# A selective scan beside two feed-forward blocks: odd decays in SBUF instead of PSUM, wide products, later attention steps

## Chip, cores, metric

The kernel runs on one core of a Trainium2 chip. The metric is the device time of one launch in microseconds, the median of several runs. TensorE is called PE here, VectorE DVE, ScalarE ACT, GpSimd POOL, SyncE SP.

## What is computed

Four samples of 512 tokens by 512 channels go through four residual steps. Cut to what matters:

```python
# 1: selective scan over the context (ctx: 4 x 512 x 256), 512 channels, 16 states
u  = silu(causal_conv4(ctx @ in_proj.T) + conv_b)            # channels x time
dt = softplus(dt_proj @ (x_proj[:16] @ u) + dt_b)
B, C = x_proj[16:32] @ u, x_proj[32:48] @ u                  # 16 x time each
state[n] = exp(-exp(A_log[:, n]) * dt) * state[n] + dt * u * B[n]      # over time
y  = (sum_n state[n] * C[n] + D * u) * silu(layernorm(x))
x += tanh(g_xattn[0]) * y.T
# 2: feed-forward 512 -> 2048 -> 512 with ternary weights and 8-bit tokens, exact gelu
x += tanh(g_ffn[0]) * bitlinear(gelu(bitlinear(layernorm(x), w1)), w2)
# 3: channel attention: q, k from ctx; A = softmax(q k^T) (512 x 512)
x += tanh(g_xattn[1]) * (layernorm(x) @ A.T)
# 4: fp32 feed-forward 512 -> 2048 -> 512 with biases, exact gelu
x += tanh(g_ffn[1]) * (gelu(layernorm(x) @ proj1.T + b1) @ proj2.T + b2)
```

## The kernel before

**Passes.** Five passes over a hand-written order of 15 slots. Pass 0 does the scan and attention matrix of sample 0, beside the quantisation of the weights. Three looped passes do steps 2 to 4 (called `rest`, sample b) beside the scan (called `scans`, sample b + 1). The last one does steps 2 to 4 of the last sample with three-product fp32. Every engine runs through the same slots; semaphores tie them.

**The scan.** Channels lie on partitions: four tiles of 128, so a state n is two half states, s = 2n + p, of two rows (q = 0, 1) of 128 x 512. `SCAN_SLOTS` puts state 0 into slot 4, two states into each of slots 5 to 11, and state 15 into slot 12. For a half state:

- POOL forms the state input `work[s % 6] = du * bcast` (L1541), four half states ahead, after it has issued the accumulation of an earlier half (`u += work`, a DMA that adds, L1552). Two accumulations into the same half of `u` follow one another, each waiting for the landing of the one before.
- ACT forms the decays, `exp(a_neg * dt)`, one instruction a row, in PSUM tile `pairs[s % 2]` (L811), once `s_hc` says that the half state two before has been multiplied. It also copies the rows of B and C, which PE has broadcast into a PSUM bank with a one-column matmul (L424), to `bcast` and `ccast` (L796).
- DVE scans each row in place in the PSUM pair, with `work` as addend (L1168, L1181), and multiplies by `ccast` back into `work`. In pass 0 and outside slots 5 to 8 the product is wide: both rows at once, 1024 elements (L1173). In slots 5 to 8 of the looped passes each row's product follows its scan (L1185), so that ACT is released row by row.

**Beside it in slots 5 to 8** of a looped pass: four up-products a slot of step 4 (`f_up`, L603, eight matmul instructions each, banks 2 and 3 in turn) and their gelus on ACT (L1026) in pairs. Gelu and exponential need different tables, so ACT loads a table four times a slot. Slots 9 to 14 have the down-products (L616).

**The attention matrix** of the next sample: in slots 6 to 9 PE forms the energies of a quarter (L481), DVE takes the maximum (L1288) after the slot's second half state, ACT the exponential with its sum (L944), DVE the reciprocal (L1348) after the third, ACT the probabilities (L949); PE transposes (L436) and ACT copies (L933) one slot later.

**Other users.** `xn` (two rows of 512, fp32) holds normalised tokens of step 4 (`norm_apply`, L1364), transposed by PE until slot 4; in slots 9 and 10 it takes the unneeded output of the statistics of `x` (L954, L958), and in slot 12 silu(layernorm(x)) (`gates_silu`, L973), with which DVE multiplies y (L1305) after `last_sum` (L1295) has waited for the last accumulations. POOL adds the second bias to the residual in slots 4 and 5 (L1609).

Of the kernel before, what the change touches and what calls it, by code (L numbers as in the profile page):

```python
# [10 lines left out]
ALU = mybir.AluOpType  # L11
# [36 lines left out]
GELU_SLOTS = (5, 6, 7, 8)  # L48
# [3 lines left out]
ATT_LAST_SLOT = 10  # L52
ZSTAT_SLOT = 10
ZS_SLOT = 12
GATE_SLOT = 13
QUANT_SLOT = 14
# [24 lines left out]
def state_at(slot, which):  # L81

    return SCAN_SLOTS[slot][which] if slot in SCAN_SLOTS else None

# [26 lines left out]
def program(nc, x_d, ctxT_d, ipw_d, xpw_d, dtw_d, pch_d, w1_d, w2_d, wqk_d, bqk_d, ffn_d, b1_d, b2_d, gate_d,  # L111
            ident_d, identb_d, pick_d, out_d):
    with ExitStack() as ctx:
# [301 lines left out]
        def _(pe):  # L415
# [249 lines left out]
            def middle(b, m, prev, scans, rest):  # L665

                if not rest:
                    pe.wait_ge(s_const, const_wait)
                    pe.wait_ge(s_ones, 2)
                if rest:  # L670
                    up1(b, 3, range(FC - 1))
                    down1(b, 1)
                    up1(b, 3, (FC - 1,))
                    norm_transpose(b, 0)
                    transpose_h(b, 2)
                if scans:
                    low_rank(m)
                if rest:
                    down1(b, 2)
                    norm_transpose(b, 1)  # L680
                    transpose_h(b, 3)
                if scans:
                    step_sizes(m, prev)
                if rest:
                    down1(b, 3)
                    attend(b, 0)
                if scans:
                    scan_bcast(m, 0, 0)
                if rest:
                    norm_transpose(b, 2)  # L690
                    attend(b, 1)
                if scans:
                    scan_bcast(m, 1, 0)
                if rest:
                    norm_transpose(b, 3)
                    attend(b, 2)
                if scans:
                    scan_bcast(m, 0, 1)

            def pass_(b, scans, rest=True):  # L700

                m, prev = (b + 1, b) if rest else (0, None)
                for slot in range(SLOTS if scans else 5):
                    if slot == 3:
                        middle(b, m, prev, scans, rest)
                    if scans and slot == QUANT_SLOT:
                        turn(m, prev)
                        continue
                    if scans and slot == 0:
                        project(m, prev, 0)  # L710
                        project(m, prev, 1)
                    if rest:
                        if slot == 0:
                            up1(b, 2)
                        if slot == 4:
                            norm_transpose(b, 4)
                            attend(b, 3)
                            norm_transpose(b, 5)
                    if scans:
                        if slot == 0:  # L720
                            project(m, prev, 2)
                        if slot == 1:
                            project(m, prev, 3)
                        bcast_next(m, slot, 0, 0)
                        if slot in ATT_SLOTS and ATT_SLOTS[slot]:
                            att_transpose(m, ATT_SLOTS[slot] - 1)
                        if slot == ATT_LAST_SLOT:
                            att_transpose(m, J - 1)
                        if slot == QK_SLOT:
                            qk_products(m, prev, 0)  # L730
                    if rest and slot == GATE_SLOT:
                        f_unit(b, slot, 0)
                    if scans and slot == GATE_SLOT:
                        gate_transposes(m, range(T))
                    if rest:
                        if slot == 1:
                            down1(b, 0)
                        if slot < 2:
                            transpose_h(b, slot)
                        if slot != GATE_SLOT:  # L740
                            f_unit(b, slot, 0)
                    else:
                        weights(slot)
                    if scans:
                        bcast_next(m, slot, 0, 1)
                        if slot in ATT_SLOTS:
                            energies(m, ATT_SLOTS[slot])
                        if slot == QK_SLOT:
                            qk_products(m, prev, 1)
                    if rest:  # L750
                        if slot == 4:
                            norm_transpose(b, 6)
                            norm_transpose(b, 7)
                        f_unit(b, slot, 1)
                    if scans:
                        bcast_next(m, slot, 1, 0)
                    if rest:
                        f_unit(b, slot, 2)
                    if scans:
                        bcast_next(m, slot, 1, 1)  # L760
                    if rest:
                        f_unit(b, slot, 3)
                if not scans:
                    tail(b)
# [13 lines left out]
            pass_(None, True, rest=False)  # L778
            with pe.Fori(0, B - 1) as i:
                pass_(i, True)  # L780
            pass_(B - 1, False)


        @block.scalar
        def _(act):
# [17 lines left out]
            def decay_half(b, s):  # L803

                n, p = divmod(s, 2)
                if n == 0:
                    act.wait_ge(s_dt, b * 2 + p + 1)
                for q in range(HALF):
                    if n:
                        act.wait_ge(s_hc, (b * HN + s - DECAYBUFS) * HALF + q + 1)  # L810
                    act.activation(pairs[s % DECAYBUFS][:, q, :], dt[:, p * HALF + q, :], ACT.Exp,  # L811
                                   scale=a_neg[:, p * HALF + q, n:n + 1]).then_inc(s_decay, 1)

            def decays(b, prev, slot, which, part):

                n = state_at(slot, which)
                if n is not None:
                    if n == 0 and part == 0:
# [3 lines left out]
                        decay_half(b, 0)  # L822
                    if n == 0 and part == 0 and prev is not None:
                        act.wait_ge(s_x3, prev * T + T)
                    if 2 * n + 1 + part < HN:
                        decay_half(b, 2 * n + 1 + part)
# [76 lines left out]
            def middle(b, m, prev, scans, rest):  # L903
                if not rest:
                    set_up()
                    for _, i, c in W_EARLY:
                        square(i, c)
                if rest:
                    gelu1(b, 3)
                    norm_copy(b, 0)  # L910
                    h_copy(b, 2)
                if scans:
                    low_rank_copy(m, prev)
                if rest:
                    norm_copy(b, 1)
                    h_copy(b, 3)
                if scans:
                    softplus(m, prev)
                    first_copy(m, prev, 0, 0)
                if rest:  # L920
                    norm_copy(b, 2)
                if scans:
                    first_copy(m, prev, 1, 0)
                if rest:
                    norm_copy(b, 3)
                if scans:
                    first_copy(m, prev, 0, 1)
# [806 lines left out]
```

## Time and profile before

| what | us |
|---|---|
| median of 3 runs (1079.14 to 1080.04) | 1079.6 |
| profiled execution, its own time | 1083.82 |
| its span | 1082.0 |
| busy: PE, DVE, ACT, POOL | 819.5, 838.0, 666.3, 574.1 |
| mean granted PE clock, of full speed | 0.882 |
| state inputs, POOL L1541, 128 | 350.6, 2.773 each |
| scans, DVE L1168 and L1181, 256 | 186.9 and 117.5 |
| products, DVE L1173 wide, 80, and L1185 narrow, 96 | 98.0 and 66.4 |
| decays, ACT L811, 256 | 166.0 |

Busy shares are means over stages that are limited in different ways, so the table names the candidates only. A mean for a POOL instruction contains the time in which it overlaps the issue of a DMA.

### The profile page before, as it was taken

To read this page: it belongs to the slowest core of one execution; us is meant where nothing else is said; L and a number is where in the kernel's file an instruction comes from. 1 tells how busy PE (TensorE), PEld (TensorE's weight loads), DVE (VectorE), ACT (ScalarE), POOL (GpSimd) and SP (SyncE) were. 2 spreads that over 40 slices of the span, in tenths; PEclk is the share of its full clock that TensorE was granted. 3 is DMA by queue.
4 is the path that set the end of the run, shared out by engine and by line. 5 is a ranking of instruction groups with operands and counts; after the bars stand their busy time and mean duration, and the time that the engine had idled before them with its cause. 6 is when DMAs were issued, how large, how long until landed. Compare 5 with 4: busy or idle time off the path is not lost.

```text
span 1082.0 us, 10856 instructions
## 1 busy us (share of the span) xinstructions
PE 819.5 (76%) x2664; PEld 403.2 (37%) x2704; DVE 838.0 (77%) x999; ACT 666.3 (62%) x969; POOL 574.1 (53%) x495
## 2 busy tenths in 40 slices
PE   4432310689699987989699988879799987887997
PEld 1110010344334334444333434443333333445886
DVE  3889868887988897787988898777888997655332
ACT  4678869375489952565589852555599851523442
POOL 0497786124797783134997781125996871232000
PEclk8655555798899998998899999998899998998999
DMA  7059985001189996201299994201398993200221
GB/s 269 0 98 206 250 170 111 0 1 40 19 187 204 199 230 172 91 8 39 45 197 203 205 235 124 98 1 39 70 207 179 220 229 86 98 0 20 98 98 59
DMA packets 51429, 129.99 MB, mean 120 GB/s; under 512 B 6304, under 2 KB 7456, under 8 KB 50864
## 3 DMA queue, kind: packets, MB, share of 16 engines
q0 software_dynamic: 17280, 62.92, 31.6%
q1 hardware_dynamic: 34096, 66.53, 17.9%
q14 instruction: 41, 0.34, 0.1%
q8 instruction: 12, 0.20, 0.1%
HBM read 62.33 MB, written 4.19 MB: 61 GB/s over the span
## 4 chain that ended last, share of the span: by engine, by line
PE 27%; DVE 22%; issue 14%; ACT 12%; DMA 11%; POOL 7%; DVEq 1%; ACTq 0%; POOLq 0%
DMA u<-work 11%; DVE pair L1168 6%; PE bank L631 4%; PE pair L631 4%; POOL work L1541 4%; PE pair L515 3%; PE bank L616 3%; DVE pair L1181 3%; PE pair L543 2%; ACT pair L811 2%; ACT L811 2%; PE pair L592 2%; PE bank L603 2%; ACT L1026 1%; PE bank L450 1%
## 5 line engine op out<-in xcount | busy, mean ns | idle before, releaser
L1541 POOL TENSOR_TENSOR work<-du,bcast 128x1024 f32<-128x1024 f32 x128 | 350.6, 2773 | 12.8 <-ACT bcast L796 7.7
L811 ACT ACTIVATE pair<-dt,a_neg 128x512 f32<-128x512 f32 x256 | 166.0, 683 | 69.7 <-DVE work L1173 53.5
L1168 DVE TENSOR_TENSOR_SCAN pair<-pair,work 128x512 f32<-128x512 f32 x160 | 186.9, 1214 | 15.4 <-ACT pair L811 11.7
L603 PE MATMUL bank<-stage,ring 128*128 128x512 f32 x384 | 174.8, 598 | 11.5 <-ACT stage L1026 3.7
L1552 POOL DMA_DIRECT2D u<-work x120 | 129.7, 1081 | 66.3 <-DMA u<-work 25.1
L1181 DVE TENSOR_TENSOR_SCAN pair<-pair,work 128x512 f32<-128x512 f32 x96 | 117.5, 1224 | 25.2 <-ACT pair L811 24.8
L424 PE MATMUL bank<-xd,pick 128*128 128x512 bf16 x108 | 48.6, 450 | 114.3 <-ACT bcast L796 74.1
L603 PEld LDWEIGHTS bank<-stage,ring 128*128 128x128 f32 x384 | 70.4, 189 | 96.0 <-issue 78.2
L1173 DVE TENSOR_TENSOR work<-pair,ccast 128x1024 f32<-128x1024 f32 x80 | 98.0, 1225 | 10.4 <-DVE pair L1168 4.7
L616 PE MATMUL bank<-ring,stage 128*128 128x512 f32 x192 | 85.4, 595 | 9.0 <-DVE stage L1406 7.7
L424 PEld LDWEIGHTS bank<-xd,pick 128*128 128x128 bf16 x128 | 12.9, 100 | 171.5 <-ACT bcast L796 110.0
L1185 DVE TENSOR_TENSOR work<-pair,ccast 128x512 f32<-128x512 f32 x96 | 66.4, 691 | 5.4
L543 PE MATMUL pair<-w2q,hx 128*128 128x512 bf16 x242 | 63.9, 416 | 7.7 <-issue 4.1
L515 PE MATMUL pair<-w1q,qT 128*128 128x512 bf16 x250 | 60.4, 387 | 12.2 <-ACT qT L979 7.1
L1192 DVE SCALAR_TENSOR_TENSOR u<-xpad,pch,u 128x512 f32<-128x512 f32 x48 | 40.6, 850 | 25.1 <-ACT u L837 23.9
L1527 POOL TENSOR_SCALAR fst<-fst 128x1 f32<-128x1 f32 x32 | 12.9, 404 | 87.5 <-DVE fst L1356 86.9
L592 PE MATMUL pair<-attT,stage 128*128 128x512 f32 x128 | 57.6, 592 | 0.0
L979 ACT ACTIVATE qT<-bank 128x512 bf16<-128x512 bf16 x16 | 9.5, 593 | 77.3 <-PE bank L502 77.3
L616 PEld LDWEIGHTS bank<-ring,stage 128*128 128x128 f32 x192 | 35.8, 190 | 51.4 <-issue 51.3
L796 ACT ACTIVATE bcast<-bank 128x512 f32<-128x512 f32 x64 | 37.2, 582 | 22.3 <-PE bank L424 17.7
L796 ACT ACTIVATE ccast<-bank 128x512 f32<-128x512 f32 x64 | 37.3, 584 | 13.7 <-PE bank L424 13.3
L616 PE MATMUL bank<-ring,hT 128*128 128x512 f32 x96 | 45.7, 621 | 0.0
(177 smaller groups left out, 1635.3 us busy)
## 6 DMA issues: line engine op xcount, KB each, us to landing
u<-work POOLq DMA_DIRECT2D x120, 512.0 KB, 5.8
ring<-ffn_dram SPq DMA_DIRECT2D x144, 256.0 KB, 4.9
ring<-ffn_dram SPq DMA_DIRECT2D x16, 512.0 KB, 3.3
xres<-x_dram SPq DMA_DIRECT2D x4, 1024.0 KB, 5.4
stage<-w_dram SPq DMA_DIRECT2D x1, 4096.0 KB, 16.5
stage<-w_dram SPq DMA_DIRECT2D x4, 1024.0 KB, 7.0
out_dram<-stage SPq DMA_DIRECT2D x16, 256.0 KB, 2.3
ctxT<-ctxT_dram SPq DMA_DIRECT2D x4, 512.0 KB, 6.5
```

The source lines that it names most:

```text
L515: last = pe.matmul(banks[4 + g % 3][:], qT[:, k, t * P:(t + 1) * P], w1q[:, k, c * 512:(c + 1) * 512], start=k == 0, stop=k == J - 1)
L543: last = pe.matmul(banks[7][:], hqT[:, f, :], w2q[:, f, :], start=f == 0, stop=f == FT - 1)
L592: last = pe.matmul(banks[ATT_BANKS[t]][:], xnT[:, k, t * P:(t + 1) * P], attT[:, k, :], start=k == 0, stop=k == J - 1)
L603: last = pe.matmul(banks[2 + f % 2][:], piece(f)[:, k * P:(k + 1) * P], xnT[:, k, :], start=k == 0, stop=k == J - 1)
L616: last = pe.matmul(banks[2 + t % 2][:], h_tile(f)[:, t * P:(t + 1) * P], piece(k), start=f == 0, stop=f == FT - 1)
L631: out = pe.matmul(bank[:], in_parts(weights), in_parts(moving), start=first and i == 0, stop=last and i == len(parts) - 1)
L811: act.activation(pairs[s % DECAYBUFS][:, q, :], dt[:, p * HALF + q, :], ACT.Exp, scale=a_neg[:, p * HALF + q, n:n + 1]).then_inc(s_decay, 1)
L1168: dve.tensor_tensor_scan(pair[:, q, :], pair[:, q, :], rows[:, q, :], 0.0, ALU.mult, ALU.add).then_inc(s_scan, 1)
L1173: dve.tensor_tensor(rows, pair[:], ccast[:, n % 2, :].unsqueeze(1).broadcast_to([P, HALF, L]), ALU.mult).then_inc(s_hc, HALF)
L1181: dve.tensor_tensor_scan(state, state, row, 0.0, ALU.mult, ALU.add).then_inc(s_scan, 1)
L1541: pool.tensor_tensor(work[:, s % SCANBUFS, :, :], du[:, p * HALF:(p + 1) * HALF, :], bcast[:, n % 2, :].unsqueeze(1).broadcast_to([P, HALF ...
L1552: pool.dma_start(u[:, p * HALF:(p + 1) * HALF, :], work[:, s % SCANBUFS, :, :], accum_op=ALU.add).then_inc(s_acc[p], 16)
```

## The change

The order of the slots before slot 4 is written out as three functions on each engine (`opening`, `between`, `closing`), in the order that the slots gave before. What differs otherwise:

- The decays of the odd half states of states 1 to 15 go to `xn` in SBUF. DVE scans from `xn` into the PSUM pair. ACT forms them at the end of the half slot before, ahead of the gelus, once `s_scan` says that the odd half before has been scanned row by row.
- All products are wide.
- The attention steps move: energies after the slot's second up-product, the maximum after the third half state, the exponential at the end of the slot and the reciprocal after the fourth half; probabilities, transposes and copy in the next slot.
- The statistics' unneeded output goes to `q1`; `gates_silu` also waits for the last scan.

```diff
+SPARE_STATES = range(1, 16)
+def spare(n, p):
+    return p == 1 and n in SPARE_STATES
...
             def decay_half(b, prev, s):
                 n, p = divmod(s, 2)
                 if n == 0:
                     act.wait_ge(s_dt, b * 2 + p + 1)
+                dst = xn if spare(n, p) else pairs[s % DECAYBUFS]
+                if spare(n, p) and n == SPARE_STATES[0] and prev is not None:
+                    act.wait_ge(s_xnT, prev * 2 * T + 2 * T)
                 for q in range(HALF):
-                    if n:
+                    if spare(n, p):
+                        if n > SPARE_STATES[0]:
+                            act.wait_ge(s_scan, (b * HN + s - 2) * HALF + q + 1)
+                    elif n:
                         act.wait_ge(s_hc, (b * HN + s - DECAYBUFS) * HALF + q + 1)
-                    act.activation(pairs[s % DECAYBUFS][:, q, :], dt[:, p * HALF + q, :], ACT.Exp,
+                    act.activation(dst[:, q, :], dt[:, p * HALF + q, :], ACT.Exp,
                                    scale=a_neg[:, p * HALF + q, n:n + 1]).then_inc(s_decay, 1)
...
+            def decays_ahead(b, prev, slot, which):
+                n = state_at(slot, which)
+                if n is not None and spare(n + 1, 1):
+                    decay_half(b, prev, 2 * (n + 1) + 1)
...
             def gates_silu(b):
                 act.wait_ge(s_emm, b * J + J)
+                act.wait_ge(s_scan, (b * HN + 2 * SPARE_STATES[-1] + 2) * HALF)
```

ACT's slot afterwards (from slot 4 on; `m` is the scan's sample):

```python
decays(m, prev, slot, 0, 0)               # nothing where the odd half is a spare one
if slot == 4: decays(m, prev, slot, 0, 1); norm_copy(b, 5)
copy_next(m, slot, 0, 0); quarter(m, slot, 0, rest)
if slot - 1 in ATT_SLOTS: energy_probs(m, ATT_SLOTS[slot - 1])
if slot == QK_SLOT: qk_copy(m, prev, 0)
if slot != 4: decays(m, prev, slot, 0, 1)
copy_next(m, slot, 0, 1); quarter(m, slot, 1, rest)
if slot - 1 in ATT_SLOTS: att_copy(m, prev, ATT_SLOTS[slot - 1])
if slot == QK_SLOT: qk_copy(m, prev, 1); norm_copy(b, 6); norm_copy(b, 7)
decays_ahead(m, prev, slot, 0)
f_gelus(b, slot, 0)
copy_next(m, slot, 1, 0); quarter(m, slot, 2, rest)
decays(m, prev, slot, 1, 1); copy_next(m, slot, 1, 1)
if slot in ATT_SLOTS: energy_exp(m, ATT_SLOTS[slot])
quarter(m, slot, 3, rest)
decays_ahead(m, prev, slot, 1)
f_gelus(b, slot, 2)
if slot == ZS_SLOT: gates_silu(m)
```

PE's: `bcast_next(0, 0)`, `f_unit 0`, `att_transpose(slot - 1)`, `bcast_next(0, 1)`, `f_unit 1`, `energies(slot)`, `bcast_next(1, 0)`, `f_unit 2`, `bcast_next(1, 1)`, `f_unit 3`. DVE's half state and slot:

```diff
-            def half_step(b, prev, n, p, wide):
+            def half_step(b, n, p):
...
+                source = xn if spare(n, p) else pairs[s % DECAYBUFS]
+                rows = work[:, s % SCANBUFS, :, :]
+                pair = pairs[s % DECAYBUFS]
                 for q in range(HALF):
                     done = (b * HN + s) * HALF + q + 1
                     dve.wait_ge(s_decay, done)
-                    dve.tensor_tensor_scan(state, state, row, 0.0, ALU.mult, ALU.add).then_inc(s_scan, 1)
...
+                    dve.tensor_tensor_scan(pair[:, q, :], source[:, q, :], rows[:, q, :], 0.0,
+                                           ALU.mult, ALU.add).then_inc(s_scan, 1)
...
-                        energy_max(m, slot)
...
+                    half(m, prev, slot, 1, 0)
+                    energy_max(m, slot)
+                    half(m, prev, slot, 1, 1)
+                    if slot in ATT_SLOTS:
+                        energy_sum(m, slot)
```

## Rows read from the trace of the kernel before

**Rows 1.** Windows: length, busy PE, PEld, DVE, ACT, POOL, clock, DMA share, GB/s.

```profile
530.20:566.00 35.80, 33.42 (x82) 14.79 (x82) 30.25 (x35) 29.32 (x43) 35.37 (x23) 0.95 0.80 170
583.90:601.80 17.90, 16.70 (x42) 7.04 (x43) 15.52 (x20) 16.61 (x25) 13.05 (x8) 1.00 0.84 173
617.60:632.10 14.50, 12.88 (x36) 5.91 (x36) 13.90 (x14) 10.46 (x21) 13.06 (x13) 1.00 1.06 256
```

**Rows 2.** Timeline of ACT in a gelu slot: start, us, instruction, [idle before].

```profile
345.12 1.28 ACT L1026 ACT_TABLE_LOAD   x1
346.42 1.27 ACT L1026 ACTIVATE hT<-bank,b 128x512 f32<-128x512 f32 x2
...
349.00 1.30 ACT L811 ACTIVATE pair<-dt,a_neg 128x512 f32<-128x512 f32 x2
350.24 0.57 ACT L796 ACTIVATE bcast<-bank 128x512 f32<-128x512 f32 x1
...
354.17 0.69 ACT L944 ACTIVATE xd<-bank,ast 128x512 f32<-128x512 f32 x1 [1.17 <-DVE ast L1288]
```

**Rows 3.** Timeline of DVE in gelu slots.

```profile
353.46 0.68 DVE L1288 TENSOR_REDUCE ast<-bank 128x1 f32<-128x512 f32 x1
...
359.56 1.23 DVE L1181 TENSOR_TENSOR_SCAN pair<-pair,work 128x512 f32<-128x512 f32 x1 [1.54 <-ACT pair L811]
360.83 0.69 DVE L1185 TENSOR_TENSOR work<-pair,ccast 128x512 f32<-128x512 f32 x1
```

**Rows 4.** Timeline of PE in a gelu slot.

```profile
339.13 3.70 PE L603 MATMUL bank<-stage,ring 128*128 128x512 f32 x8 [0.88 <-ACT hT L1026]
342.84 0.39 PE L424 MATMUL bank<-xd,pick 128*128 128x512 bf16 x1
...
351.35 1.13 PE L481 MATMUL bank<-xpad 128*128 128x512 f32 x2
```

**Rows 5.** Single lines of DVE: duration in ns, least, median, most.

```profile
L1168 DVE TENSOR_TENSOR_SCAN pair<-pair,work x160: 1199/1208/1232, 51.5 to 891.7; 128x512 f32<-128x512 f32 x160
...
L1173 DVE TENSOR_TENSOR work<-pair,ccast x80: 1223/1225/1226, 53.9 to 893.0; 128x1024 f32<-128x1024 f32 x80
...
L1225 DVE TENSOR_TENSOR dt<-dt,hT x4: 1224/1224/3247, 47.1 to 752.2; 128x1024 f32<-128x1024 f32 x4
...
L1192 DVE SCALAR_TENSOR_TENSOR u<-xpad,pch,u x48: 744/751/2344, 12.9 to 709.4; 128x512 f32<-128x512 f32 x48
```

**Rows 6.** Timelines of POOL and DVE where both work in SBUF.

```profile
45.97 3.25 POOL L1541 TENSOR_TENSOR work<-du,bcast 128x1024 f32<-128x1024 f32 x1 [2.42 <-DVE du L1227]
47.07 3.25 DVE L1225 TENSOR_TENSOR dt<-dt,hT 128x1024 f32<-128x1024 f32 x1
...
225.59 2.32 POOL L1602 TENSOR_SCALAR du<-du,fst 128x2048 f32<-128x2048 f32 x1 [9.45 <-DVE fst L1373]
...
287.15 0.54 DVE L1364 TENSOR_SCALAR xn<-stage,fst 128x512 f32<-128x512 f32 x1
287.37 0.87 POOL L1504 TENSOR_SCALAR u<-u,pch 128x512 f32<-128x512 f32 x1
287.60 0.92 DVE L1364 TENSOR_SCALAR xn<-stage,fst 128x512 f32<-128x512 f32 x1
```

**Rows 7.** Timelines of POOL and DVE, gelu slot and slot 9.

```profile
360.75 2.35 POOL L1541 TENSOR_TENSOR work<-du,bcast 128x1024 f32<-128x1024 f32 x1 [1.24 <-ACT bcast L796]
...
375.52 1.21 DVE L1168 TENSOR_TENSOR_SCAN pair<-pair,work 128x512 f32<-128x512 f32 x1
376.64 1.20 DVE L1168 TENSOR_TENSOR_SCAN pair<-pair,work 128x512 f32<-128x512 f32 x1
376.82 2.67 POOL L1541 TENSOR_TENSOR work<-du,bcast 128x1024 f32<-128x1024 f32 x1
```

**Rows 8.** Waits of DVE: total us, times, longest.

```profile
DVE u L1295 <- DMA u<-work: 10.9, 6, 2.8
```

**Rows 9.** Timeline of POOL in pass 0.

```profile
92.71 0.88 POOL L1552 DMA_DIRECT2D u<-work  x1 [3.00 <-DMA u<-work]
```

More of the change, by code:

```diff
@@ L51 @@
 ATT_SLOTS = {6: 0, 7: 1, 8: 2, 9: 3}
-ATT_LAST_SLOT = 10
 ZSTAT_SLOT = 10
@@ L700, in pass_, with opening @@
[L700 to L706, printed above, removed]
+            def opening(m):
+                for j in range(J):
+                    project(m, None, j)
+                pe.wait_ge(s_const, const_wait)
+                pe.wait_ge(s_ones, 2)
+                low_rank(m)
+                step_sizes(m, None)
+                scan_bcast(m, 0, 0)
+                scan_bcast(m, 1, 0)
+                scan_bcast(m, 0, 1)
@@ L707, in pass_ @@
+            def pass_(b, rest=True):
+                m, prev = (b + 1, b) if rest else (0, None)
+                if rest:
+                    between(b, m)
+                else:
+                    opening(m)
+                for slot in range(4, SLOTS):
+                    if slot == QUANT_SLOT:
                         turn(m, prev)
                         continue
-                    if scans and slot == 0:
-                        project(m, prev, 0)
-                        project(m, prev, 1)
+                    bcast_next(m, slot, 0, 0)
+                    if slot == QK_SLOT:
+                        qk_products(m, prev, 0)
@@ L712, in pass_ @@
                     if rest:
[L713 to L730, printed above, removed]
@@ L742, in pass_ @@
                     else:
                         weights(slot)
[L744 to L751, printed above, removed]
+                    if slot - 1 in ATT_SLOTS:
+                        att_transpose(m, ATT_SLOTS[slot - 1])
@@ L901, in tail, with opening @@
                         weight_high(b, f + 2)
[L903 to L927, printed above, removed]
+            def opening(m):
+                for j in range(J):
+                    project_copy(m, None, j)
+                silu_u(m)
+                set_up()
+                for _, i, c in W_EARLY:
+                    square(i, c)
+                low_rank_copy(m, None)
+                softplus(m, None)
+                first_copy(m, None, 0, 0)
+                first_copy(m, None, 1, 0)
+                first_copy(m, None, 0, 1)
@@ L1467, in pass_ @@
+                dve_m.start()
+                if rest:
+                    between(b, m)
+                else:
+                    opening(m)
+                for slot in range(4, SLOTS):
+                    half(m, prev, slot, 0, 0)
+                    if rest and slot == 4:
+                        norm_apply(b, 6)
+                        norm_apply(b, 7)
+                    half(m, prev, slot, 0, 1)
                     if rest and (slot, 0) in FOURTH_SLOTS:
                         fourth(b, FOURTH_SLOTS[slot, 0])
[L1469 to L1474 removed]
+                    half(m, prev, slot, 1, 0)
+                    energy_max(m, slot)
+                    half(m, prev, slot, 1, 1)
+                    if slot in ATT_SLOTS:
+                        energy_sum(m, slot)
+                    mixer_last(m, prev, slot)
@@ L1679, in _ @@
-            pass_(None, True, rest=False)
+                pool_m.start()
+                if rest:
+                    between(b, m)
+                else:
+                    softplus_log(m)
+                    start_sum(m, None)
+                for slot in range(4, SLOTS):
+                    if rest and slot == 5:
+                        bias(b, 2)
+                    half(m, prev, slot, 0, 0)
+                    if rest and slot == 4:
+                        bias(b, 0)
+                    if rest and slot == 5:
+                        bias(b, 3)
+                    half(m, prev, slot, 0, 1)
+                    if rest and slot == 4:
+                        bias(b, 1)
+                    if not rest:
+                        weights(slot)
+                    half(m, prev, slot, 1, 0)
+                    half(m, prev, slot, 1, 1)
+                    mixer_last(m, slot)
```

536 lines of the change are left out of this document (261 added, 275 removed).

## Prediction

> **What bounds the kernel now.** I read the windows by stage first. In one of the three looped passes, slots 5 to 8, each with two states (four half states) beside four up-products and their gelus, take 17.9 us in slot 8 (slots 5 and 6 together 35.8), and no engine is idle for much of that: PE 16.7, ACT 16.6, DVE 15.5. Slot 10 takes 14.5 us, 3.62 per half state, with DVE at 13.9 [rows 1]. So DVE sets slots 9 to 12; what sets a gelu slot has to be found in the queues.
>
> ACT's timeline of a gelu slot gives steps from start to start: table load 1.29, two gelus 1.28, a half state's two exponentials 1.24, a copy 0.48, the energies' exponential 0.80 [rows 2]; the probabilities take about as long as that, 0.73. Four loads, two gelu pairs, four half states, four copies, an attention copy, probabilities and exponential make 16.6 us. The missing 1.2 is the wait for DVE's maximum [rows 2]. DVE itself waits 1.54 for decays [rows 3]. ACT and DVE thus feed each other through the two PSUM pairs: this is the wait the change is aimed at. PE waits 0.88 for a gelu [rows 4].
>
> **The change, part by part, if nothing new collides.** *Wide products:* two narrow ones of 0.69 [rows 3] become one of 1.225 [rows 5], so the 96 narrow ones of the three passes, as 48 wide, save 7.5 us of DVE time, but only where DVE sets the pace. *Decays ahead:* instruction count and table loads stay the same (exponentials, gelus, exponentials, gelus in a slot), so ACT's 16.6 us stays the floor. *Attention:* the same instructions in other places, nothing added. *Moved statistics output* to q1: free, q1 is idle then.
>
> The new order closes another ring. From the first gelu at a slot's end it is 0.74 until PE starts, f_up 3.71, transposes 0.43, broadcast 0.24, f_up 3.47, energies 0.96, broadcast 0.24, f_up 3.47, last broadcast 0.49 to its landing [rows 4] (an f_up right behind a broadcast is 3.47 from start to start); then on ACT the copy 0.48, energies' exponential 0.80, decays ahead 1.24, table load 1.29 [rows 2]. Sum 17.6 us against 17.9. Laid out from slot 4 (the table loads and decays of the first slot included), slot 9 starts 2.4 us earlier than before. After it DVE's 3.62 per half state is unchanged. Three passes: 7 us.
>
> Queues behind new waits: on ACT the odd decays now wait for the previous odd half's scans (s_scan), and the gelus, and behind them PE's next up-products, are queued behind that. gates_silu now waits for the last scan; then a table load and two silus (1.3 + 1.4) against DVE's product and sum (2.3): 0.5 us per pass at most. POOL's instructions and DMAs (30 accumulations a pass) keep their order.
>
> **The collision.** The scan of an odd half today reads a PSUM pair and work. Afterwards it reads xn and work, both in SBUF, while POOL's state input reads du and bcast. What such a pair does is in the trace. A DVE tensor_tensor with both inputs in SBUF, 1.224 us at its shortest and in the middle, took 3.25 us when POOL's state input had been issued before it [rows 5, 6]; and that state input, else 2.35 [rows 7], took 3.25, held up by the DVE instruction before. In the convolution, all operands in SBUF, one step of 0.75 took 2.34 beside POOL's rounding [rows 5, 6]. Against that, 160 scans and 80 wide products with one input in PSUM lie within 1.199 to 1.232 and 1.223 to 1.226 us, with POOL at work beside most of them [rows 5]. So the two exclude each other for whole instructions when DVE has two inputs in SBUF. The Trainium skill says the same (SBUF — State Buffer, "Who interferes with whom": a DVE instruction with two SBUF inputs contends with a GpSimd instruction that reads SBUF); the trace agrees, 3.25 against 1.224. Without rule and rows alike the sum would be the 1072 of the first rival. No scan of that kind is in the trace: its price lies between 0 and a whole state input, 2.34, for each scan; I take the lock, since the nearest rows are two-input instructions too.
>
> Who goes first? Two DVE instructions in a row do not keep POOL out: between norm_apply's two, POOL's waiting multiply of 0.87 came through, and the second took 0.92 where the first took 0.54 [rows 6]. So first come, first served. A product's end releases both the next scan and POOL's accumulation with the state input behind it: scans at 375.52 and 376.64, the input at 376.82 [rows 7]. On time, the input thus comes 0.18 us after the second scan and merely waits ("a near miss", some 0.5 us per state); if the first scan starts 0.2 us late, or energy_max (0.68 [rows 3]) sits before it, the input slips between the scans and the second waits 2.34 ("a hit"). A near miss leaves POOL late by half a microsecond, which makes the next one a hit: they alternate.
>
> *Slots 5 and 6.* POOL is behind after the bias adds (35.4 of 35.8 us busy [rows 1]) and always has something waiting. Odd halves 3, 5, 7, 9 then pay 1.3 + 2.35, 1.25 + 1.55, 0.5 + 2.35 and 2.35: 11.6 us. Eight half states of 3.6, a wait of 1.3 for the first decays, a maximum of 0.6 and these give 42.3 us against 35.8. ACT's gelus wait with it, as their decays stand before them: slot 7 starts 6.4 later.
>
> *Slots 7 and 8.* State inputs of even halves wait for ACT's broadcast copy (today 1.24 us [rows 7]) and so come after both odd scans: no hits. DVE needs 15.0 us, catches up in slot 7 (16.3), and slot 8 takes the ring's 17.6. 33.9 against 35.8: slot 9 starts 4.5 later.
>
> *Slots 9 to 12.* I get hits at halves 21, 25 and 29 (the first through energy_max, the others by alternation): 7.0, with near misses 0.5. POOL's last inputs, for halves 30 and 31, come late behind its gate statistics, so that one of them still meets half 29; after that it has none left. Today DVE waits at the end for the accumulations, 10.9 us in six waits, two in each of the three passes [rows 8]; 3.6 a pass; later half states give the accumulations that time, 3.1 with the silus' 0.5 taken off. Net 4.4.
>
> *Pass 0.* Thirteen odd halves collide too, but POOL itself waits there for accumulations (3.00 us and more [rows 9]), and runs 6 to 12 us behind DVE; most is swallowed. I count 4 us (0 to 15).
>
> Sum: 3 × (4.5 + 4.4) + 4 = 30.7 us, 31 in whole microseconds. The profiled execution took 1083.8 us (span 1082.0, 1.8 around it), 4.2 above the median of 1079.6; the same 31 on the median gives **1110 us**.
>
> **Rivals.** *No collision for scans* (faster side): then the ring gain alone stands: 7 us, 1072. For it: no scan with two SBUF inputs was seen. Against: three kinds of two-input or fast DVE instruction collide. It decides if odd scans stay at 1.21 us. *The pair of scans stays together*: no hits, only waits of up to 1.2 for a running input; slots 5 and 6 lose about 3, later slots 0.5 per state, the end gives 3 back: 1080 to 1086. The deciding point is whether POOL comes between two queued scans. *Every odd half is hit* up to half 27: three more hits in slots 9 to 11 (7.0), 4 in slots 7 and 8 beyond their slack of 2.6, and 5 in pass 0: 38 more, 1148. *The changed order alone costs*: PE's last broadcast of a slot stands behind energies and an up-product; if ACT and PE drift, the 17.6 becomes 18.5, 10 us over the passes; it would show without any long scan.
>
> **Chances and range.** Collision with alternation 0.60 (1095 to 1128 of its own); every half hit 0.10; scans together 0.13, half of it within what I call the same; no collision 0.14; order alone 0.03. A difference below 0.2% (2 us) cannot be told from none here: faster 0.14, same 0.06, slower 0.80. The range, 1076 to 1138, leaves out most of the no-collision case and the upper half of the worst one.
>
> **What would show it.** By form, the scans with xn as input: maximum near 3.5 us, mean above 1.8, scans with pair inputs still 1.21. State inputs up to 2.34 + 1.2. Half states of slots 9 to 11 in pairs of 7.7 and 9.5 us instead of 7.2. Slot 5 plus 6 at 42 us, slot 7 at 16. Narrow products gone; ACT waiting on s_scan before its odd decays in slots 5 and 6. I would be wrong if odd scans lie at 1.21 us, or if pass 0 grew by more than 15 us.

## The result, and the profile after

The changed kernel takes 1203.5 us (four runs, 1201.7 to 1204.9) against 1079.8: a ratio of 1.1125, 95% interval 1.1067 to 1.1182. It is 11% slower, 124 us where 31 were forecast, and above the range's 1138. The profiled execution took 1201.7 us, with a span of 1199.9.

The page of the changed kernel: busy time and share by engine, then the costliest groups.

```profile
PE 850.7 (71%) x2704; PEld 416.6 (35%) x2704; DVE 1000.3 (83%) x951; ACT 672.1 (56%) x969; POOL 589.1 (49%) x495
...
L1589 POOL TENSOR_TENSOR work<-du,bcast 128x1024 f32<-128x1024 f32 x128 | 345.1, 2698 | 4.8 <-DVE du L1248 4.8
L1200 DVE TENSOR_TENSOR_SCAN pair<-xn,work 128x512 f32<-128x512 f32 x120 | 318.5, 2698 | 5.6 <-ACT xn L831 5.6
...
L1205 DVE TENSOR_TENSOR work<-pair,ccast 128x1024 f32<-128x1024 f32 x128 | 156.8, 1225 | 18.6 <-DVE pair L1200 9.1
L1200 DVE TENSOR_TENSOR_SCAN pair<-pair,work 128x512 f32<-128x512 f32 x136 | 158.7, 1213 | 3.5 <-ACT pair L831 3.0
L831 ACT ACTIVATE xn<-dt,a_neg 128x512 f32<-128x512 f32 x120 | 84.4, 718 | 90.5 <-DVE pair L1200 90.3
```

The single line of the scans: duration in ns, least, median, most.

```profile
L1200 DVE TENSOR_TENSOR_SCAN pair<-pair,work x136: 1199/1210/1232, 51.7 to 1016.3; 128x512 f32<-128x512 f32 x136
L1200 DVE TENSOR_TENSOR_SCAN pair<-xn,work x120: 1199/1390/12783, 64.9 to 1019.9; 128x512 f32<-128x512 f32 x120
```

The 136 scans from PSUM kept their time; the 120 from `xn` went from 1.21 us [rows 5] to a mean of 2.70, with one of 12.8. That is 120 × (2.698 - 1.21) = 179 us more in the scans. DVE's busy time grew by 162: busy time counts once where two rows overlap, and two narrow products had cost more than a wide one. POOL's state inputs have not grown: 2.70 after, 2.77 before. One side pays all. ACT's decays waited 90 us for those scans, and the gelus and PE's up-products with them. PE's granted clock fell to 0.85 (0.88 before) and its busy time rose by 31 us; in the first kernel below, where only the scans' source differs, the clock is 0.877 and the loss is gone.

Windows of pass 2, cut at the starts of half states 2, 10, 18 and 31 (columns as in [rows 1]):

```profile
587.13:637.41 50.28, 37.65 (x86) 16.19 (x84) 47.73 (x27) 30.57 (x44) 35.91 (x23) 0.87 0.64 131
637.41:677.72 40.31, 32.85 (x84) 14.31 (x84) 39.11 (x31) 33.74 (x49) 26.23 (x16) 1.00 0.78 170
677.72:744.10 66.38, 54.22 (x115) 23.51 (x116) 64.38 (x45) 34.05 (x62) 44.88 (x40) 0.85 0.80 183
```

The same stretches of the kernel before are 35.86, 35.75 and 49.79 us long. DVE is now busy for 95 to 97% of all three. From start to start of half state 0, pass 0 grew by 25.6 us (232.0 to 257.6), the first two looped passes by 31.1 and 33.7, and the third with all behind it by 27.2. No stretch was spared.

Half state 3, where the largest loss sits. Single rows of DVE, POOL and ACT's timelines; an x1 row is one instruction:

```profile
591.88 12.62 DVE L1200 TENSOR_TENSOR_SCAN pair<-xn,work 128x512 f32<-128x512 f32 x1 [0.99 <-ACT xn L831]
604.42 1.20 DVE L1200 TENSOR_TENSOR_SCAN pair<-xn,work 128x512 f32<-128x512 f32 x1
...
591.75 1.54 POOL L1657 TENSOR_TENSOR stage<-stage,b 128x512 f32<-128x512 f32 x1
592.97 1.19 POOL L1600 DMA_DIRECT2D u<-work  x1
593.59 2.94 POOL L1589 TENSOR_TENSOR work<-du,bcast 128x1024 f32<-128x1024 f32 x1
...
598.95 3.24 POOL L1589 TENSOR_TENSOR work<-du,bcast 128x1024 f32<-128x1024 f32 x1
601.25 2.15 POOL L1657 TENSOR_TENSOR stage<-stage,b 128x512 f32<-128x512 f32 x1
...
604.54 0.72 ACT L831 ACTIVATE xn<-dt,a_neg 128x512 f32<-128x512 f32 x1 [8.61 <-DVE pair L1200]
```

A scan of 1.21 us waited until POOL had worked off all that was ready in its queue: two state inputs and four bias additions, the last of which ended at 603.40, 1.10 us before the scan did. They stand back to back but for 0.30 us (593.29 to 593.59), in which only an accumulation was being issued; the scan did not get its turn there either.

The steady state, slot 6, single rows of DVE and POOL:

```profile
609.75 1.23 DVE L1205 TENSOR_TENSOR work<-pair,ccast 128x1024 f32<-128x1024 f32 x1 [0.20 <-DVE pair L1200]
610.89 1.39 DVE L1200 TENSOR_TENSOR_SCAN pair<-xn,work 128x512 f32<-128x512 f32 x1
612.19 3.82 DVE L1200 TENSOR_TENSOR_SCAN pair<-xn,work 128x512 f32<-128x512 f32 x1
...
608.53 2.65 POOL L1589 TENSOR_TENSOR work<-du,bcast 128x1024 f32<-128x1024 f32 x1
611.64 0.89 POOL L1600 DMA_DIRECT2D u<-work  x1 [0.46 <-issue]
612.26 2.65 POOL L1589 TENSOR_TENSOR work<-du,bcast 128x1024 f32<-128x1024 f32 x1
```

The product's end at 610.98 releases both sides. The first scan meets the tail of the input before (608.53 + 2.65 = 611.18) and takes 1.39 instead of 1.21. The second is thereby issued 0.07 us ahead of the next input, not 0.18 as forecast, and ends when that input has ended: 3.82 us. In this way every odd half of slots 5 to 8 behind half 3 is hit, 1.39 + 3.82 or, behind a maximum, about 4.6 in all, against 2.42 without a hit. Slot 8 takes 20.2 us and slot 10 21.0 (657.56 to 677.72 and 697.88 to 718.89, from scan to scan), against 17.90 and 14.50 [rows 1].

### The profile page after: what moved, and what is told of

It reads as the page before. It is cut to its first block, busy times and chain, and to the rows that moved or that the text cites. A ratio compares the mean times of both kernels' runs of the same rounds, so it can differ in the third digit from the quotient of the medians.

```text
span 1199.9 us, 10941 instructions
## 1 busy us (share of the span) xinstructions
PE 850.7 (71%) x2704; PEld 416.6 (35%) x2704; DVE 1000.3 (83%) x951; ACT 672.1 (56%) x969; POOL 589.1 (49%) x495
## 4 chain that ended last, share of the span: by engine, by line
PE 31%; DVE 29%; issue 13%; ACT 6%; POOL 2%; DVEq 1%; ACTq 0%; POOLq 0%
DVE pair L1200 18%; PE bank L607 7%; PE bank L635 4%; PE pair L635 4%; PE pair L519 3%; PE bank L620 3%; PE pair L547 2%; PE pair L596 2%; ACT L1082 2%; PE bank L454 1%; DVE hx L1438 1%; DVE fst L1430 1%; DVE fst L1413 1%; PE bank L477 1%; DVE u L1213 1%
## 5 line engine op out<-in xcount | busy, mean ns | idle before, releaser
L1200 DVE TENSOR_TENSOR_SCAN pair<-xn,work 128x512 f32<-128x512 f32 x120 | 318.5, 2698 | 5.6 <-ACT xn L831 5.6
L607 PE MATMUL bank<-stage,ring 128*128 128x512 f32 x384 | 185.2, 627 | 56.0 <-ACT stage L1082 41.0
L1600 POOL DMA_DIRECT2D u<-work x120 | 116.4, 970 | 177.9 <-DVE work L1205 148.9
L1205 DVE TENSOR_TENSOR work<-pair,ccast 128x1024 f32<-128x1024 f32 x128 | 156.8, 1225 | 18.6 <-DVE pair L1200 9.1
L1200 DVE TENSOR_TENSOR_SCAN pair<-pair,work 128x512 f32<-128x512 f32 x136 | 158.7, 1213 | 3.5 <-ACT pair L831 3.0
L831 ACT ACTIVATE xn<-dt,a_neg 128x512 f32<-128x512 f32 x120 | 84.4, 718 | 90.5 <-DVE pair L1200 90.3
L428 PE MATMUL bank<-xd,pick 128*128 128x512 bf16 x128 | 57.2, 447 | 109.4 <-ACT bcast L810 66.1
L831 ACT ACTIVATE pair<-dt,a_neg 128x512 f32<-128x512 f32 x136 | 88.3, 682 | 76.9 <-DVE work L1205 60.8
L620 PE MATMUL bank<-ring,stage 128*128 128x512 f32 x192 | 97.4, 663 | 17.9 <-ACT hx L1082 9.2
L440 PE MATMUL bank<-ident,xd 128*128 128x128 f32 x64 | 13.2, 343 | 42.3 <-ACT xd L1004 42.3
```

Source lines behind the costliest of these rows:

```text
L607: last = pe.matmul(banks[2 + f % 2][:], piece(f)[:, k * P:(k + 1) * P], xnT[:, k, :], start=k == 0, stop=k == J - 1)
L620: last = pe.matmul(banks[2 + t % 2][:], h_tile(f)[:, t * P:(t + 1) * P], piece(k), start=f == 0, stop=f == FT - 1)
L831: act.activation(dst[:, q, :], dt[:, p * HALF + q, :], ACT.Exp, scale=a_neg[:, p * HALF + q, n:n + 1]).then_inc(s_decay, 1)
L1200: dve.tensor_tensor_scan(pair[:, q, :], source[:, q, :], rows[:, q, :], 0.0, ALU.mult, ALU.add).then_inc(s_scan, 1)
L1205: dve.tensor_tensor(rows, pair[:], ccast[:, n % 2, :].unsqueeze(1).broadcast_to([P, HALF, L]), ALU.mult).then_inc(s_hc, HALF)
L1600: pool.dma_start(u[:, p * HALF:(p + 1) * HALF, :], work[:, s % SCANBUFS, :, :], accum_op=ALU.add).then_inc(s_acc[p], 16)
```

## The experiments

Theory 1 is the collision: the whole loss is the wait of scans with two SBUF inputs for POOL. The other theories differ from run to run. Twelve kernels were run. Where a kernel has two runs only, its interval is the wider for it.

**Taking the collision away.** The first kernel leaves all in place but the source that DVE reads:

```diff
-dve.tensor_tensor_scan(pair[:, q, :], source[:, q, :], rows[:, q, :], 0.0, ALU.mult, ALU.add)
+dve.tensor_tensor_scan(pair[:, q, :], pair[:, q, :], rows[:, q, :], 0.0,
+                       ALU.min if spare(n, p) else ALU.mult, ALU.add)
```

> The changed kernel with one operand changed: DVE scans the odd half states of states 1 to 15 from the PSUM pair (combined with min, so that values stay finite) instead of xn; ACT still writes the odd decays to xn and every wait stays. The odd decays are thus left out of the result. Theory 1 (a scan with both inputs in SBUF and POOL's SBUF-reading instructions exclude each other, and DVE is the one that waits): odd scans back at 1.21 us each, total 1068 to 1085 us. Rival 2 (the slot order, the later attention steps and the odd decays' waits on s_scan cost the time): 1180 us or more, with DVE idle instead of long scans. Rival 3 (both): in between, 1100 to 1160.

1072.4 us, ratio 0.988 [0.978, 0.999]. The group of its scans on the page:

```profile
L1200 DVE TENSOR_TENSOR_SCAN pair<-pair,work 128x512 f32<-128x512 f32 x256 | 299.1, 1214 | 16.3 <-ACT pair L831 8.3 <-ACT xn L831 4.3 <-POOL work L1589 2.3
```

All 256 scans take 1.21 us, and 131 us are gone with one operand. Nothing else in the change, the waits on `s_scan` and on the last scan included, costs anything that these two runs (1067.4 and 1077.5) could show.

The second keeps the order and the wide products, with the odd decays in PSUM and in their old place:

```diff
-SPARE_STATES = range(1, 16)
+SPARE_STATES = ()
...
-                act.wait_ge(s_scan, (b * HN + 2 * SPARE_STATES[-1] + 2) * HALF)
```

> The changed kernel with no spare states: odd decays go to the PSUM pairs as before; wide products everywhere and the later attention steps stay. Theory 1: 1070 to 1085 us, faster or equal to before, since gelu slots are then set by the ring through PE and ACT, 17.6 to 17.9 us a slot. Rival 2 (order costs): 1130 us or more.

1070.4 us, 0.987 [0.980, 0.994]. Its pass 2, same cuts:

```profile
528.01:561.27 33.26, 32.08 (x81) 14.26 (x81) 28.76 (x27) 28.53 (x42) 33.26 (x23) 0.97 0.81 171
561.27:595.52 34.25, 32.83 (x84) 14.39 (x85) 29.63 (x30) 33.60 (x49) 28.42 (x18) 1.00 1.02 222
595.52:645.75 50.23, 44.43 (x112) 19.29 (x113) 47.47 (x44) 35.78 (x66) 41.49 (x39) 1.00 0.96 224
```

The third puts the odd decays alone into the kernel before, formed in their old place, with its order and its narrow products:

```diff
+def spare(n, p):
+    return p == 1 and n >= 1
...
-act.activation(pairs[s % DECAYBUFS][:, q, :], ...
+act.activation((xn if spare(n, p) else pairs[s % DECAYBUFS])[:, q, :], ...
```

> The kernel before with one part of the change: odd decays of states 1 to 15 written to xn at their old place in ACT's queue (statistics output to q1, silu after the last scan), narrow products and old attention steps kept. Theory 1: the odd scans are as long as in the changed kernel, 2.4 to 2.9 us on average, total 1160 to 1210 us. Rival 2: 1075 to 1090 us.

1209.0 us, 1.114 [1.104, 1.125]. The loss is there without the new order. The lines of its scans, wide and narrow branch:

```profile
L1175 DVE TENSOR_TENSOR_SCAN pair<-xn,work 128x512 f32<-128x512 f32 x72 | 168.1, 2379 | 3.4 <-ACT xn L816 3.4
L1188 DVE TENSOR_TENSOR_SCAN pair<-xn,work 128x512 f32<-128x512 f32 x48 | 128.4, 2674 | 19.9 <-ACT xn L816 18.5 <-POOL work L1548 1.0
```

**The two gains apart.** Wide products in slots 5 to 8 alone (the kernel before, `GELU_SLOTS = ()`):

> The kernel before with wide products in all slots, nothing else. By the reasons of the prediction ACT's decays for the next half are released later by a wide product, and the queues of ACT and DVE feed each other: 1076 to 1086 us, no gain worth naming. If DVE's busy time alone counted, 7.5 us less: 1072.

1083.0 us, 0.9986 [0.9960, 1.0011]: nothing. And the attention order alone, on the changed kernel with no spare states and with each row's narrow product behind its scan in slots 5 to 8:

> The kernel before with the new slot order alone: attention steps later, odd decays at their old place in PSUM, narrow products in slots 5 to 8. If the later attention steps give the 9 us that the order-only kernel gained: 1068 to 1076 us; if the wide products give them: 1077 to 1084 us.

1067.9 us (1066.1 to 1069.5), 0.986 [0.983, 0.990], faster than both kernels. Its slots 5 and 6 take 33.94 us and 7 and 8 take 33.58, against 35.86 and 35.75. ACT's wait for DVE's maximum, 13.5 us in 11 waits in the kernel before, is not in the list of its waits any more:

```profile
ACT bcast L811 <- PE bank L429: 25.1, 16, 3.0
...
ACT ccast L811 <- PE bank L429: 14.7, 10, 3.0
...
ACT xpad L994 <- PE bank L478: 10.9, 4, 3.2
```

**Are the hits independent?** Only the odd halves of states 1 to 8 in `xn`, then only those of 9 to 15:

```diff
-SPARE_STATES = range(1, 16)
+SPARE_STATES = range(1, 9)      # the other kernel: range(9, 16)
```

> The changed kernel with the decays of the odd half states of states 1 to 8 alone in xn (slots 5 to 8); those of states 9 to 15 are in PSUM, formed in their old place. Against the version with none in xn (1070), the changed kernel's segments of pass 2 (halves 2 to 10, 10 to 18, 18 to 31) are 17.0, 6.1 and 16.2 us longer. Theory 1 (each odd half's scans are hit by the state input that POOL issues beside them, whatever came before): the first two segments keep their loss and the third returns to about 50 us; 3 x 23 us and about 14 us of pass 0: 1140 to 1158. Theory 2 (POOL, set back once in slots 5 and 6 by bias adds and hits, carries the collisions through the rest of the pass): the third segment stays well over 50 us with scans from PSUM too, since POOL itself is late: 1165 or more.

> The mirror of it: the decays of the odd half states of states 9 to 15 alone in xn (slots 9 to 12), those of states 1 to 8 in PSUM. Theory 1: segments about 33.5, 34.5 and 66 us, every odd scan pair of slots 9 to 12 at about 5.2 us; 3 x 16 and about 13 of pass 0: 1125 to 1137. Theory 2 (the lateness from slots 5 and 6 is needed for the hits): most odd scans of slots 9 to 12 stay at 1.21 us, 1075 to 1095. The two kernels' losses over 1070 add up to that of the changed kernel (133) within 15 us if the hits are independent.

1145.0 us, 1.060 [1.057, 1.063], and 1115.6 us, 1.031 [1.028, 1.035]. Pass 2 of the two, same cuts:

```profile
561.11:611.39 50.28, 37.65 (x86) 16.18 (x84) 47.73 (x28) 30.57 (x44) 35.90 (x23) 0.87 0.64 131
611.39:651.69 40.30, 33.20 (x85) 14.61 (x86) 39.10 (x30) 34.97 (x50) 26.20 (x16) 1.00 0.79 170
651.69:702.82 51.13, 44.46 (x109) 19.20 (x108) 47.25 (x45) 33.55 (x63) 42.36 (x40) 0.97 0.98 224
```

```profile
549.94:583.79 33.85, 32.96 (x82) 14.80 (x81) 28.77 (x28) 28.69 (x42) 33.35 (x23) 0.94 0.82 170
583.79:618.04 34.25, 32.94 (x86) 14.39 (x85) 29.63 (x30) 33.61 (x50) 28.34 (x18) 1.00 1.01 220
618.04:684.43 66.39, 52.51 (x121) 22.76 (x120) 64.38 (x43) 35.44 (x64) 44.80 (x40) 0.90 0.80 182
```

Each stretch has either the changed kernel's length or the hit-free one, to within 1 us (50.28, 40.30, 51.13; 33.85, 34.25, 66.39). Theory 2, POOL's lateness carried on, is refuted. The second kernel came out 9 us under its range, mostly since its pass 0 lost 7 us, not 13 (half state 0 of the next pass starts at 292.3 against 285.7). The losses over 1070.4 add up to 75 + 45 = 120 of 133, so at most a tenth of the loss needs both groups of hits.

**How POOL holds the scans.** Each state input as two instructions of 512 elements:

> The changed kernel with each POOL state input split into two instructions of 512 elements (about 1.2 us each) right behind one another. Theory 1a (POOL keeps the port while it has an instruction ready; DVE gets it only in a gap of POOL's queue): the second odd scan still waits for both, 3.6 to 3.9 us, first odd half of a pass still 12 us and more, total 1195 to 1215 us. Theory 1b (one instruction of POOL, then DVE's): the wait of the second scan halves to about 1.2 us, the longest scan falls below 4 us, total 1130 to 1165 us.

1188.2 us, 1.095 [1.084, 1.105]: 7 under the range of 1a, far above that of 1b. The longest scan takes 14.1 us, and on-time odd halves still 5.3 us a pair; only those behind a maximum fell from 4.6 to 3.5. A scan that waits for POOL mostly doesn't get the gap between two instructions that stand ready.

The four bias additions moved from slots 4 and 5 to slots 7 and 8:

> The changed kernel with POOL's four bias adds (1.53 us each) moved from slots 4 and 5 to slots 7 and 8, where POOL idles. Theory 1a (POOL keeps the port as long as its queue has an instruction ready, and a DVE scan waits for all of them): the longest scan of a looped pass falls from 12.8 to 4 to 8 us, total 12 to 25 us below the changed kernel. Theory 1b (a scan waits for one instruction): the longest scan was another wait, nothing changes by more than 5 us.

1198.5 us, 1.107 [1.102, 1.112]. The longest scan of pass 2 fell from 12.62 to 8.21 us: it now waits for three state inputs back to back, which end at 601.45 where the scan ends at 602.55. But halves 11 and 15 wait for the additions in their new place, 6.4 us a pair instead of 5.2: the gain in all was 5 us, not 12 to 25.

**Putting POOL's inputs where they do no harm.** Two state inputs in a row, issued once the odd half's scans are over:

```diff
+                    if p == 0:
+                        if n < NS - 1:
+                            accumulate(b, n, p)
+                        return
+                    if s + AHEAD - 1 < HN:
+                        pool.wait_ge(s_scan, (b * HN + s + 1) * HALF)
+                        state_input(b, prev, s + AHEAD - 1)
                     if n < NS - 1:
                         accumulate(b, n, p)
                     if s + AHEAD < HN:
                         state_input(b, prev, s + AHEAD)
```

> The changed kernel, with POOL's two state inputs of a state held back until the odd half's two scans are done (POOL waits on s_scan), so that they run beside the product and the next even half, which read one operand from PSUM. Theory 1 (the collision is the whole loss): most odd scans at 1.21 us, slots 9 to 12 near 7.3 us a state, first odd half of a pass still held up by the bias adds; total 1085 to 1120 us. Rival 2 (writing to xn or reading from it is slow in itself): odd scans stay at 2.7 us on average, total 1190 us or more.

1125.4 us, 1.038 [1.034, 1.042], 5 above the range:

```profile
L1200 DVE TENSOR_TENSOR_SCAN pair<-xn,work 128x512 f32<-128x512 f32 x120 | 215.4, 1838 | 5.4 <-ACT xn L831 5.4
```

The waits in the scans fell from 179 to 75 us. What stays sits at half 3 (up to 8.6 us in one scan), beside the gate statistics and, 22 of the 75, in pass 0.

**Who goes first?** Waits that are met long before, put into POOL's queue to make the input some tenths of a microsecond later:

```diff
                     if s + AHEAD < HN:
+                        if p == 0:
+                            for _ in range(12):          # the other kernel: 20
+                                pool.wait_ge(s_const, const_wait)
                         state_input(b, prev, s + AHEAD)
```

> The changed kernel with twelve more waits, all met long before, in POOL's queue between an accumulation and the state input behind it, in the calls that follow an even half's product. In the trace of the changed kernel POOL's queue takes about 0.09 us from one such instruction to the next, and some six are hidden behind the 0.62 us of the accumulation's issue, so the input would be issued about 0.5 us later: 0.5 us after the second scan of the odd half instead of 0.07. Theory 1 (who comes first by a margin has the port: the scans of seven profiles that met an input issued less than 0.35 us after their start were mostly held, those with an input 0.4 us or more behind never): the steady hits vanish, odd scans mostly at 1.21, the input waits up to 0.8 instead; the waits behind the bias adds and the gate statistics stay; total 1085 to 1130, as with the aligned inputs. Theory 2 (POOL has priority over a scan whatever the order): nothing gained, 1195 to 1215 with the mean of the odd scans at 2.6 to 2.7.

> The same with twenty such waits: the input is issued about 1.2 us later, at the end of the second scan. Theory 1: as with twelve, no hit in the steady state, and less waiting of the input, but POOL's queue is longer by 0.7 us a state; 1085 to 1135, within 15 us of the kernel with twelve waits. Theory 2: 1195 to 1220.

1144.3 us, 1.050 [1.042, 1.058], and 1144.9 us, 1.054 [1.047, 1.060]. Both miss: 14 and 10 above theory 1's ranges, 50 below theory 2's. The rows show why. Twelve waits, single rows of DVE and POOL in pass 2:

```profile
612.33 1.33 DVE L1200 TENSOR_TENSOR_SCAN pair<-xn,work 128x512 f32<-128x512 f32 x1
613.58 1.20 DVE L1200 TENSOR_TENSOR_SCAN pair<-xn,work 128x512 f32<-128x512 f32 x1
...
621.43 3.39 DVE L1200 TENSOR_TENSOR_SCAN pair<-xn,work 128x512 f32<-128x512 f32 x1
...
613.08 0.89 POOL L1600 DMA_DIRECT2D u<-work  x1 [0.52 <-issue]
613.77 3.16 POOL L1589 TENSOR_TENSOR work<-du,bcast 128x1024 f32<-128x1024 f32 x1
...
621.13 2.58 POOL L1589 TENSOR_TENSOR work<-du,bcast 128x1024 f32<-128x1024 f32 x1
```

By the rows' starts the waits delayed the input by little, from 0.07 to 0.19 us behind the second scan's, not 0.5. Yet the on-time inputs stopped holding scans: the scan at 613.58 took 1.20 us and the input waited instead (3.16 against 2.65). Where a maximum stands ahead of the odd half, the input was issued 0.30 us before the second scan, and the scan was held (3.39). So POOL does not simply rank over DVE, and moving its input a little in its queue was worth 59 us. With twenty waits an on-time input comes 0.53 us after the scan, which in pass 2 frees only half 13 more and shortens the waits of half 29; the odd halves of slots 6, 8 and 9 behind a maximum are held still.

All single rows of the nine profiles with scans from `xn` show how far the order of the starts goes. Of 960 such scans, 422 started with POOL's big instructions (over 1 us) idle and met one that was issued between 0.5 us before and 1.3 us after their own start. Issued more than 0.05 us before the scan, 125 of 125 held it. From 0.05 before to 0.31 after, 84 held it and 63 did not. Later than 0.31 after, none of 150 did.

Inside that margin the difference of the starts does not decide. Two cases against it, each with the second scan of an odd half and the input; the first is from the kernel with late states, the second from pass 0 of the kernel with twelve waits:

```profile
622.86 3.99 DVE L1200 TENSOR_TENSOR_SCAN pair<-xn,work 128x512 f32<-128x512 f32 x1
623.10 2.65 POOL L1589 TENSOR_TENSOR work<-du,bcast 128x1024 f32<-128x1024 f32 x1
...
126.90 1.20 DVE L1200 TENSOR_TENSOR_SCAN pair<-xn,work 128x512 f32<-128x512 f32 x1
126.88 3.37 POOL L1589 TENSOR_TENSOR work<-du,bcast 128x1024 f32<-128x1024 f32 x1
```

An input that starts 0.24 us after the scan holds it, and one that starts 0.02 before it waits. What does separate them is the place behind an accumulation. Of the second scans inside the margin, 77 were held, and in all 77 the input started 0.61 or 0.62 us after the start of an accumulation's issue, with nothing between; of the 52 that were not held none was of that kind. With twelve waits the input mostly starts 0.69 after the issue (613.08 to 613.77), in the case above 0.63. The queue's own records suggest why: in the changed kernel the last one before the input ends at 611.82, ahead of the scan at 612.19, though the input itself starts at 612.26, behind the issue; with twelve waits it ends at 613.77, after the scan's start at 613.58. So an input may count from when POOL's queue hands it over, and not from its start in the trace. That is a guess from these records, and five first scans of half 29 in pass 0, held though the last record ended 0.2 us after their start, don't fit it; no run was made to test it.

## Why the prediction was wrong

Right were the direction, the collision itself and the side that pays. The step that failed is **"Who goes first?"**: its reading of the order from the starts, its alternation, and a wait of one input at most. Each looped pass was to lose 8.9 us and pass 0 4; they lost 31.1, 33.7, 27.2 (the third with all behind it) and 25.6.

- *"On time, the input comes 0.18 us after the second scan and merely waits."* It comes 0.07 us after in the changed kernel, since the first scan has just been pushed back 0.18 us by the input before, and it wins. At 0.18 it would most likely have won too: directly behind an accumulation's issue inputs held the second scan when they started up to 0.30 us after it, at 0.17 to 0.18 in three cases of the source-only kernel. The near miss that the sum counts at 0.5 us is a hit of 2.8 (5.21 for the pair against 2.42).
- *"They alternate."* They don't: a hit costs DVE time and POOL none, so POOL is on time again for the next odd half, and the next one is hit. In the kernel with twelve waits, where on-time inputs do lose, pairs of 2.5 and 4.6 us do take turns in slots 6 to 9, but by the maximum ahead of each slot's second odd half, not by a lateness.
- *First come, first served* came from one place, where POOL slipped between two DVE instructions [rows 6]. The other way round it hardly holds: DVE mostly doesn't get between POOL's queued instructions.
- **"Slots 5 and 6"**, 42.3 us forecast, 50.28 measured. Half 3 alone pays 11.4 us in one scan where the sum has 1.3 + 2.35. The reason is the previous point: POOL has four bias additions and two inputs ready, and the scan waits for all.
- **"Slots 7 and 8"**, no hits and 33.9 us forecast, 40.31 measured. I had the inputs wait for ACT's broadcast copy, as before; with DVE late, the copy is long done, and every odd half is hit. The hit-free kernel takes 34.25 here, so the rest of that step was right.
- **"Slots 9 to 12"**: three hits forecast, five of the seven odd halves held (19, 21, 23, 25 and 29), and 66.38 us against 49.79 from half 18 to 31. The time given back at the end of the pass was right in kind: DVE's 10.9 us of waits for accumulations [rows 8] no longer stand among its waits, but they were 3.6 a pass against 16.6.
- **"Pass 0"**, 4 us forecast, 25.6 measured, over the 15 named as the sign of an error. The waits of POOL's that I took for slack there did not help the scans, which waited 38 us.
- The time of "no collision", 1072, was met: 1072.4 with the operand in PSUM, 1070.4 with the old decays. That was in part luck. The kernel before took 1084.8 beside these two, so the gain was 12 and 14 us, not the 7 of the sum. Its source was wrong too: wide products are worth nothing, and the attention order gives all of the 1.4%: ACT's wait of 1.17 us for the maximum [rows 2], 13.5 in all, is gone, and the ring that I had laid out at 17.6 us a slot comes out shorter (34.25 us for slots 7 and 8).
- The rival "every odd half is hit", at 1148, named what happened in slots 5 to 8 and was still 55 us short: it too had no wait longer than one input, and 5 us for pass 0.

What a microsecond in a scan costs can be read from the runs: the time over 1070.4, divided by the scans' excess over 1.21 us, is 133 of 179 in the changed kernel, 75 of 113 and 45 of 69 in the kernels with early and late states, 118 of 167 with split inputs, 55 of 75 with aligned ones, 74 of 114 and 75 of 97 with twelve and twenty waits. So 65 to 77% of the waits reach the end.

The Trainium skill (SBUF — State Buffer, "Who interferes with whom") says of a DVE mode that locks the pair that whoever issues first gets it for the whole instruction. The rows of the nine profiles agree for scans with two SBUF inputs, outside a margin of about 0.3 us in the traced starts (125 of 125 held before it, none of 150 behind it). That one side keeps the other out over several queued instructions, 12.6 us for a scan of 1.21, goes further than the page does.

Open is whether the hand-over from POOL's queue is what decides inside the margin, where 84 scans were held and 63 not, and why a scan that waits is passed over between two ready instructions of POOL. The best version is the attention order alone, 1067.9 us; an order of POOL's queue under which `xn` would pay was not found, and even hit-free the decays ahead showed no gain (1072.4 with them, in two runs 10 us apart, 1070.4 without).

## What to carry to other kernels

Before an operand of DVE's goes from PSUM to SBUF, count the instructions whose two inputs are then both in SBUF, and what POOL has ready beside each. Price each at all that POOL has queued without a gap, not at one instruction. When two engines are released by the same event, their order repeats in every round, so a margin of some tenths of a microsecond is lost or won every time: don't average over it, and don't read it from the starts alone where POOL's instruction stands right behind the issue of a DMA.

## What was new about the hardware

- `tensor_tensor_scan` with both inputs in SBUF waits for POOL's instructions like a two-input `tensor_tensor`; with one input in PSUM none of the 136 took over 1.232 us.
- POOL's back-to-back instructions kept a waiting scan out for 11.4 us (12.6 in all), and for 12.9 (14.1 in all) when the inputs were split into halves.
- POOL's issue of an accumulating DMA did not hold a scan: 610.89 to 612.28 has the issue at 611.64 in it, but its 0.18 us are the tail of the input before. In the nine profiles 56 scans from `xn` that were under way beside such an issue alone took 1.20 to 1.23 us.
- A state input right behind an accumulation's issue started 0.61 to 0.62 us after it and held a scan that had started up to 0.30 us before the input (77 of 77 such second scans in the margin; of the 52 with any other input none was held).
- A wait that is already met costs POOL's queue little: twelve of them between issue and input moved the input's start from 0.62 to 0.69 us behind the issue, twenty to 1.04. Against the second scan's start that is 0.12 and 0.46 us later.
